# Moving output-projection passes, a normalisation and three copies between queues of an attention step, and spreading the last softmax denominators by matrix products

## The reference, cut to what matters

```python
x = x + attention(layernorm(x), ctx, ctx)     # x and ctx: 16 sequences x 256 tokens x 512
x = x + ffn(layernorm(x))                     # 512 -> 2048 -> 512, quantised weights and activations

# attention: 16 heads of 32 columns, rotary positions, window of 128 tokens to either side
scores = q @ k.T * sqrt(32); masked outside the window
attn = softmax(scores)
out = attn @ v;  return out @ wo.T + wo_b
```

## Time and profile before

| | us |
|---|---|
| median of 3 runs | 1254.26 |
| lowest and highest of them | 1252.21, 1255.16 |
| the profiled execution, its own time | 1251.07 |
| span of the profiled execution, first to last instruction | 1249.3 |
| TensorE busy, share of the span | 91% |
| VectorE busy | 79% |
| ScalarE busy | 51% |
| GpSimd busy | 29% |

### The profile page before, as it was taken

How to read it: one execution, slowest core, us unless ns; L and a number is a source line. 1 busy time by engine, 2 the same in 40 slices (tenths; PEclk the granted TensorE clock), 3 DMA queues, 4 the chain that set the end, 5 groups by cost and what they waited for, 6 DMA issues and landing times.

```text
span 1249.3 us, 23318 instructions
## 1 busy us (share of the span) xinstructions
PE 1138.1 (91%) x7776; PEld 759.7 (61%) x7776; DVE 981.0 (79%) x2527; ACT 639.6 (51%) x1000; POOL 366.4 (29%) x540
## 2 busy tenths in 40 slices
PE   5889999999999899999999665999999979999997
PEld 5767777787777688677768443444444434444443
DVE  6769989989988988988899545666666678888885
ACT  5254355335435534543553243555655458777774
POOL 1136336344533634453363220000000030112220
PEclk9889999999999999999999787999999989999999
DMA  8453575566456447545644711455554400567762
GB/s 270 110 143 106 158 178 137 139 183 155 108 161 177 131 134 194 140 120 164 177 119 114 218 56 69 160 206 198 208 188 143 152 0 35 186 224 249 219 207 92
DMA packets 96055, 191.44 MB, mean 153 GB/s; under 512 B 13392, under 2 KB 24912, under 8 KB 95952
## 3 DMA queue, kind: packets, MB, share of 16 engines
q1 hardware_dynamic: 95952, 190.14, 51.5%
HBM read 89.43 MB, written 44.04 MB: 107 GB/s over the span
## 4 chain that ended last, share of the span: by engine, by line
PE 38%; DVE 31%; issue 24%; DMA 3%; SPq 2%; ACT 2%; POOL 0%; DVEq 0%; ACTq 0%; POOLq 0%
PE bank L792 17%; DVE bank L1063 6%; PE bank L514 4%; PE bank L515 4%; PE bank L516 4%; DVE bn L1024 3%; PE bank L597 2%; DVE roped L1089 2%; DVE neg_max L1104 2%; DVE rt L1086 2%; DVE row_max L1063 2%; DVE rt L1087 2%; DVE x_res L1056 1%; PE bank L526 1%; PE bank L581 1%
## 5 line engine op out<-in xcount | busy, mean ns | idle before, releaser
L1063 DVE CUSTOM_DVE_ANT_0 bank<-bank,mask 128x256 f32<-128x256 f32 x512 | 201.4, 454 | 54.6 <-PE bank L597 48.0
L792 PE MATMUL bank<-wout_int,g_hi 128*128 128x512 bf16 x512 | 195.8, 382 | 8.8 <-DVE g_lo L1336 8.7
L792 PE MATMUL bank<-wout_int,g_lo 128*128 128x512 bf16 x512 | 195.6, 382 | 0.0
L761 PE MATMUL bank<-qT_hi,win_int 128*128 128x512 bf16 x512 | 194.2, 379 | 1.4 <-DVE qT_lo L1254 1.4
L761 PE MATMUL bank<-qT_lo,win_int 128*128 128x512 bf16 x512 | 194.1, 379 | 0.0
L864 ACT ACTIVATE probs<-bank 128x512 f32<-128x512 f32 x256 | 142.4, 603 | 52.8 <-PE bank L631 48.3
L1381 POOL TENSOR_SCALAR_AFFINE_SELECT probs<-probs 128x256 f32<-128x256 f32 x256 | 109.1, 430 | 82.9 <-ACT probs L864 78.6
L1336 DVE TENSOR_TENSOR g_lo<-h_int,g_hi 128x512 f16<-128x512 f32 x128 | 104.3, 815 | 35.6 <-ACT g_hi L991 34.3
L597 PE MATMUL bank<-k_st,q_st 96*128 96x256 f32 x512 | 98.4, 306 | 25.7 <-DVE row_max L1063 19.3
L1374 POOL TENSOR_TENSOR x_res<-x_res,wo_b 128x512 f32<-128x512 f32 x32 | 42.0, 1332 | 243.9 <-DMA x_res<-in_x 231.1
L964 ACT ACTIVATE h_ring<-bank,b_in,g_scale 128x512 f32<-128x512 f32 x96 | 73.5, 778 | 75.2 <-PE bank L761 58.1
(11 more groups left out here) (146 smaller groups left out, 2666.2 us busy)
## 6 DMA issues: line engine op xcount, KB each, us to landing
hidden_scratch<-h_ring SPq DMA_DIRECT2D x96, 256.0 KB, 2.0
h_ring<-hidden_scratch SPq DMA_DIRECT2D x96, 256.0 KB, 3.0
k_st<-k_hi SPq DMA_DIRECT2D x128, 128.0 KB, 2.5
q_st<-q_hi SPq DMA_DIRECT2D x128, 128.0 KB, 2.4
xq<-x_scratch SPq DMA_DIRECT2D x16, 1024.0 KB, 6.2
x_ln<-in_x SPq DMA_DIRECT2D x16, 512.0 KB, 4.5
ctx_raw<-in_ctxT SPq DMA_DIRECT2D x16, 512.0 KB, 4.9
k_st<-k_lo SPq DMA_DIRECT2D x64, 128.0 KB, 2.7
```

The costliest lines, as they stand in the source:

```text
L761: mm = pe.matmul(bank[f % 4][:], win_int[:, c, f * P:(f + 1) * P], part[:, par, c], start=c == 0 and part is qT_hi, stop=c == KC - 1 and p ...
L792: mm = pe.matmul(bank[4 * par + u][:], part[:, f % 4, u * P:(u + 1) * P], wout_int[:, f], start=f == 0 and part is g_hi, stop=f == FC - 1 ...
L1063: dve.tensor_tensor_reduce(sc, sc, mask[:, (1 - qb) * P:(1 - qb) * P + S], 1.0, NEG, ALU.add, ALU.max, row_max[:, qb, n:n + 1]).then_inc(m ...
```

## The change

- **The table of output passes.** 16 of the 24 passes are issued by the table. Before, 11 of them stood ahead of the first narrow piece and five behind it, one each behind heads 8, 9, 10, 12 and 13. Now all 16 stand ahead of it, two each behind heads 4 to 7.
- **ScalarE's queue.** `ctx_hi(b + 2)` moves from behind exponential 8 to behind exponential 7. `norm1` moves from the start of the step that uses it to behind exponential 11 of the step before (so `norm1(b + 2)` in step b, and `norm1(1)` ahead of step 0). `oT_copy(b, 0)` and `centre(b - 1, 0)` move behind exponential 15.
- **VectorE's queue.** `ln1(b + 2)` moves ahead of `quantise_win(b)`.
- **The last sequence.** `spread_shares(15)`, its two DMAs, is taken out. In its place TensorE multiplies four constant 128x128 matrices (`pick`, one for each i, with a one where row 32 * (col // 32) + i meets column col) with `den_r`, and VectorE multiplies `oT` by the products out of PSUM. The constant is loaded by one DMA of 256 KB in the first step.

```diff
 # SyncE
             load_ctx(2)
+            sp.dma_start(pick[:], t["c_pick"]).then_inc(pick_in, 16)
...
-            spread_shares(NB - 1)
             load_xres(NB - 1)
 # TensorE
-                for n, count in enumerate((1, 2, 2, 3, 1, 1, 1, 0, 1, 1, 1, 0, 1, 1, 0, 0)):
+                for n, count in enumerate((1, 2, 2, 3, 2, 2, 2, 2, 0, 0, 0, 0, 0, 0, 0, 0)):
...
             steps(pe, step)
+            pe.wait_ge(pick_in, 16)
+            pe.wait_ge(den_done, NB)
+            for half in range(2):
+                pe.wait_ge(oT_out, 2 * NB - 1 + half)
+                for a in range(2):
+                    mm = pe.matmul(pv_bank[half][:, a * S:(a + 1) * S], pick[:, 2 * half + a], den_r, start=True, stop=True)
+                mm.then_inc(share_mm, 1)
 # ScalarE
             ctx_hi(1)
+            norm1(1)
             def step(b, par, has_c, has_o, has_proj, has_xt):
-                if has_proj:
-                    norm1(b + 1)
...
-                    if n == 8 and has_xt:
+                    if n == 7 and has_xt:
                         ctx_hi(b + 2)
-                    if n == 12:
-                        oT_copy(b, 0)
-                    if n == 13 and has_o:
-                        centre(b - 1, 0)
+                    if n == 11 and has_xt:
+                        norm1(b + 2)
+                oT_copy(b, 0)
+                if has_o:
+                    centre(b - 1, 0)
                 if has_o:
                     centre(b - 1, 1)
 # VectorE
-                quantise_win(b)
                 if has_xt:
                     ln1(b + 2)
+                quantise_win(b)
...
             invert(NB - 1)
-            normalise(NB - 1, 0)
-            normalise(NB - 1, 1)
+            for half in range(2):
+                dve.wait_ge(share_mm, half + 1)
+                part = oT[:, 2 * half:2 * half + 2].rearrange("p i t -> p (i t)")
+                dve.tensor_tensor(part, part, pv_bank[half][:], ALU.mult).then_inc(onorm, 1)
```

More of the change, by code:

```diff
@@ L77, in constants @@
     hot = np.tile((np.arange(HOT) % NC4 == NC4 - 1).astype(np.float32), (P, 1))
+    row, col = np.arange(P)[:, None], np.arange(P)[None, :]
+    pick = np.stack([row == DK * (col // DK) + i for i in range(NC4)], 1).astype(np.float32)
     sel = np.zeros((P, H), np.float32)
@@ L80, in constants @@
         sel[MROW + h, h] = sel[MROW + H + h, h] = 1.0
-    return {"c_rope": rope, "c_mask": mask, "c_sel": sel, "c_hot": hot, "c_ident": np.eye(P, dtype=np.float32)}
+    return {"c_rope": rope, "c_mask": mask, "c_sel": sel, "c_hot": hot, "c_pick": pick, "c_ident": np.eye(P, dtype=np.float32)}
 def build(nc, t):
@@ L139, in build @@
         hot = sb("hot", [P, HOT], F32, pa)
+        pick = sb("pick", [P, NC4, P], F32, pa)
         x_ln = sb("x_ln", [P, 2, D], F32, pa)
@@ L194, in build @@
         share = probs[:, 0:2].rearrange("p n k q -> p (n k q)")
-        c_in, rope_in, ident_in, b_out_in = sem("c_in"), sem("rope_in"), sem("ident_in"), sem("b_out_in")
+        c_in, rope_in, ident_in, pick_in, b_out_in = (sem(n) for n in ("c_in", "rope_in", "ident_in", "pick_in", "b_out_in"))
         w_in = {n: sem("in_" + n) for n in ("wk", "wq", "wv", "wo")}
@@ L215, in build @@
         st_mm, exp_done, p_ready, pv_mm = sem("st_mm"), sem("exp_done"), sem("p_ready"), sem("pv_mm")
-        den_mm, den_done, den_out, share_in, oT_out, onorm = (
-            sem(n) for n in ("den_mm", "den_done", "den_out", "share_in", "oT_out", "onorm"))
+        den_mm, den_done, den_out, share_in, share_mm, oT_out, onorm = (
+            sem(n) for n in ("den_mm", "den_done", "den_out", "share_in", "share_mm", "oT_out", "onorm"))
         xres_b, res_done = sem("xres_b"), sem("res_done")
```

## The result

| | before | after |
|---|---|---|
| median, us | 1253.24 (4 runs, 1250.35 to 1255.16) | 1296.24 (4 runs, 1293.58 to 1301.75) |
| profiled execution, us (its span) | 1251.07 (1249.3) | 1301.75 (1300.0) |
| mean granted TensorE clock | 0.970 | 0.957 |

The ratio after to before is 1.0351, with a 95% interval of 1.031 to 1.0391. The forecast was 1300 us. What has to be shown is whether it came out for its reasons.

What follows compares the result with a forecast made beforehand. TensorE, busy 41.23 of 43.56 us a step, was taken to bound it, VectorE setting the transposes' start. 1251.07 + 52 (13 x 4.0) - 1 - 4 = 1298 profiled, 1301 as median, said as 1300; range 1290 to 1320.

Steps and rivals of the forecast that it cites:

- The stall: ScalarE stands behind exponential 11 until ln1, slowed by GpSimd, is done: 1.8 us a step, 23 us over steps 1 to 13.
- the late start of 2.6 us: After ScalarE's wait for ln1, the next step's scores on TensorE start at 350.45 in place of 347.81.
- the cushion: TensorE's gap of 0.82 us ahead of the transposes of x, which the late scores were to use up.
- the three that were read: TensorE's gaps in one step: 0.80 us before the first narrow piece, 0.32 before the last, 0.82 before the transposes of x.
- TensorE everything else: The reading that VectorE decides when the transposes start and TensorE decides the rest of the step.
- The clock: TensorE's 3.6 us gap before head 15 halves its clock for 4.5 us of work: 2.2 us a step, bounds 0 and 4.6.
- The rival with falls by turns: ScalarE's wait comes, but TensorE's clock stays up or falls only in some steps: 1272, up to 1290; chance 0.24.
- quantise_win, nothing: On VectorE behind ln1, done near 346.5 while w_transposes wants it near 348.1: no cost.
- The passes: Five output passes moved ahead of TensorE's first narrow piece, partly into 0.80 us of idle time: gain about 0.1 us, no more.
- Step 15, +0.3: The last step waits for exponentials 8 and 12 without fillers: 0.3 us longer.
- The tail, -4: Last sequence, from invert to the multiplications: products replace the DMA wait, 7.0 us becomes 2.5 to 3; -4 us (-2.5 to -5).
- The signs named ahead: Profile marks: norm1 idle about 3 us, TensorE gap over 3, clock below 1.00, steps 46 to 48 us, den_scratch wait gone.

Runs made afterwards that it cites:

- the first two runs: The changed kernel with norm1 alone put back at the start of the step that uses it, 1262.14 us; with norm1 and ln1 both put back, 1251.94 us.

## Why the prediction was right, point by point

**The stall, right, with one term too small and one reading wrong.** The small operations (6.33 us for about 6.4), the wait of `norm1` (3.03 for 3.2) and the gap ahead of head 15 (3.22 for 3.6) came as worked out, and the run with short subtractions shows that GpSimd is the cause. Of the path, the late start of 2.6 us fits: it is the 2.3 us below and the cushion of 0.3. What failed is the cushion: the gap ahead of the transposes was read off one step as 0.82 us, and that was step 7, the largest of all. Over the steps of the trace of before it is 0.15 to 0.57 us elsewhere, mostly 0.47, of which 0.15 is issue and doesn't go. So the cushion is worth about 0.3 us a step, and the stall costs 2.6 - 0.3 = 2.3 us a step, not 1.8. The filled gap measures just this: 46.08 - 43.81 = 2.3. Two gaps of step 6 that also wait for VectorE, 0.27 us ahead of a score and 0.40 ahead of `max_transposes`, were not among the three that were read, so "TensorE everything else" went too far.

**The clock, right, a little too dear.** 2.2 us a step were taken, with bounds of 0 and 4.6; measured are 1.5 by the medians and 1.9 by the profiled executions. The 4.5 us at half rate that were estimated are 3.4 in ten of the 13 steps, 6.8 in two and none in one. The two misses cancel, which is luck: 4.0 predicted and 4.1 measured. So is part of the last step of the sum. The profiled execution was forecast at 1298 us and took 1301.75, and 3.2 us were added for the median, which then lay 5.5 us below the profiled one. The rival with falls by turns came in one step, step 2; `norm1` behind exponential 12 shows it, with smaller gaps. The Trainium skill (TensorE: Matmul & The Clock Gate, Part 1) has the two levels, and the traces agree: nothing between 0.50 and 1.00 but where a stretch holds some of each.

**quantise_win, nothing, right only under cover.** Its 0.0 us of waiting in the changed kernel is what was said, but the due time of 348.1 that it was held against was one that the stall had itself put off. With the stall gone TensorE waits 1.06 us a step for it, 13.8 in all, and `ln1`'s place costs 10.2 us by the medians of the first two runs. The working had taken the stall's own delay as the cover and not said so.

**The passes, wrong in sign, small.** Alone they cost some 3 us, where a gain of 0.1 us a step was said. The working looked at TensorE only. Its own gaps do get smaller, by 11.1 - 7.8 = 3.3 us in all, but in the kernel before VectorE sets the start of the transposes, so there was nothing to win there. What was lost shows in VectorE's chain (5.51 us for 5.17) and in step 15. The trace of the table alone is 9.0 us longer than that of the kernel before, 5.8 of it in steps 1 to 13 and 2.8 in step 15, and the medians differ by 3.8; so the share of each is not settled by one profile.

**Step 15, +0.3 for +2.5, open.** It took 44.25 us in the trace of before and 44.1 with `norm1` moved alone, but 45.68 with the shares alone, where nothing ahead of the tail was changed but the constant's load in the first step, and 47.0 with the table. It hangs on a DMA behind 2.5 MB of loads: VectorE waits for it 7.71 us in the kernel before, 8.57 in the changed one, 8.41 with the shares alone and 9.25 with the table. That is 0.9 of the 2.5 us. The half-rate stretch of this step lasts 27.3 us in place of 23.9, which would be worth up to 1.7 more by an estimate at half rate. No run puts either down to one edit.

**The tail, -4 for -4.2 in the stretch named and -5.3 behind the last step.** The four products took 1.97 us (taken 1.7), at full clock; that is 0.49 us for one, above the 0.43 that was to be the most at that clock. The 1.1 us beyond go with the output passes: all 24 ran at full clock in the changed kernel, and in the kernel before, behind 5.69 us of waiting, the first seven at half. The edit alone is worth 3.5 us.

**The signs named ahead.** The wait of 3 us by `nmr`, the gap of over 3 us, the low clock in the exponential half, steps of 47.4 to 48.1 us in ten of 13, GpSimd's rows and the missing wait for `den_scratch` all showed.

## What to carry to other kernels

Before an operation moves ahead of others in an in-order queue, ask when its own input is done, and what stands behind it: here 1.5 us of work that nobody was waiting for held up four exponentials, and through one of them the whole step. A chain of tiny VectorE operations costs what GpSimd lets it cost, so put it where GpSimd is idle, or has bands alone, rather than where VectorE has a slot. And read a cushion over all steps, not in one; a price of nothing for an edit is only good while the cover named for it lasts.

## What the runs showed of the hardware that was not expected

- **The clock can fall in nearly every period of a loop.** A gap of 3.22 us in a step of 47.4 us was followed by 3.4 or 6.8 us at half rate in 12 of 13 steps and by nothing in one, and a gap of 4.21 us by 3.4 and 6.8 us by turns in all 13. Gaps of about 1.1 and 0.7 us with 0.4 us of work between them did it in four steps of 13 and not in the other nine. Filling the gap of 3.2 us with products that nobody reads kept the clock at 1.00 and won 20 us.
- **One small VectorE operation per GpSimd instruction.** An operation on 128x2 numbers took 0.16 to 0.20 us free, 0.32 or 0.33 beside a band (0.41 us) and 0.66 or 0.67 beside a subtraction of 128x256 (0.73 us), and ended with it; the 13 took 2.70, 3.84, 5.2 and 6.33 us in four kernels with the same chain.
- **A small DMA behind large loads.** Two issues of a round trip of 128 KB stood 7.25 us apart behind 2.5 MB of loads in the queue, and 2.77 us apart ahead of them.
- **Full fp32 products.** Four of 128x256 on a 128x128 operand, in the trace eight instructions, took 1.97 us, just behind 1.93 us in which TensorE was idle.
